# Attention stage: value matmuls of two k tiles issued together on even steps, denominator groups behind them, two reciprocals to a step

## What is computed

```python
att = jnp.einsum('bhgqd,bhkd->bhgqk', q, k) / scale
att = jax.nn.softmax(att, axis=-1)
y = jnp.einsum('bhgqk,bhkd->bhgqd', att, v)
```

## Time and profile before

| | |
|---|---|
| median of the runs | 3878.38 us |
| profiled execution, its own time | 3881.62 us |
| span in the trace | 3879.9 us |
| attention (first turn to last denominator group) | from 371 to 2257 us of the span |
| TensorE busy over the whole span | 3690.1 us (95%) |
| VectorE, ScalarE, GpSimd busy | 2415.0, 1732.0, 1627.1 us |

### The profile page before, as it was taken

How to read it: one execution, slowest core, us unless ns; L and a number is a source line. 1 busy time by engine, 2 the same in 40 slices (tenths; PEclk the granted TensorE clock), 3 DMA queues, 4 the chain that set the end, 5 groups by cost and what they waited for, 6 DMA issues and landing times. The chain is left out here.

```text
span 3879.9 us, 59156 instructions
## 1 busy us (share of the span) xinstructions
PE 3690.1 (95%) x19372; PEld 2401.0 (62%) x19372; DVE 2415.0 (62%) x4160; ACT 1732.0 (45%) x3071; POOL 1627.1 (42%) x549
## 2 busy tenths in 40 slices
PE   6998999999999999999999979799999999979889
PEld 4776444444444444444444358688888888868888
DVE  6433787777787777777777558544444444445554
ACT  3110466665666656666666633222222222125555
POOL 1111587787787777788788820000000000001110
PEclk8998899999999999999999999899999999999999
DMA  6654100101001010100100035711011111042121
GB/s 226 184 180 133 34 12 23 34 15 32 23 15 31 23 24 23 34 15 20 34 23 4 9 106 181 205 28 28 28 31 35 28 28 27 17 132 70 45 64 45
DMA packets 186866, 218.32 MB, mean 56 GB/s; under 512 B 29268, under 2 KB 148820, under 8 KB 182808
## 3 DMA queue, kind: packets, MB, share of 16 engines
q1 hardware_dynamic: 168488, 153.92, 14.3%
q0 software_dynamic: 15856, 59.52, 4.8%
q10 hardware_dynamic: 2304, 2.10, 0.2%
HBM read 152.70 MB, written 62.27 MB: 55 GB/s over the span
## 5 line engine op out<-in xcount | busy, mean ns | idle before, releaser
L689 DVE TENSOR_REDUCE att_chunk_max<-att_scores 128x1 f32<-128x512 f32 x2048 | 1284.7, 677 | 411.4 <-PE att_scores L760 404.2
L675 ACT ACTIVATE att_exp<-att_scores_T 128x512 f32<-128x512 f32 x2048 | 1122.3, 595 | 734.6 <-PE att_scores_T L774 716.3
L646 POOL TENSOR_TENSOR att_exp_pair<-att_exp 128x2048 f32<-128x2048 f32 x256 | 1169.5, 4579 | 440.7 <-ACT att_exp L675 440.7
L774 PE MATMUL att_scores_T<-att_q_stack,att_k_stack 98*128 98x512 f32 x2048 | 863.0, 424 | 13.1 <-ACT att_exp L675 9.6
L760 PE MATMUL att_scores<-att_k_stack,att_q_stack 96*128 96x512 f32 x2048 | 798.4, 436 | 40.2 <-DVE att_chunk_max L689 27.2
L774 PEld LDWEIGHTS att_scores_T<-att_q_stack,att_k_stack 98*128 98x128 f32 x2048 | 386.4, 189 | 497.8 <-ACT att_exp L675 290.4
L785 PE MATMUL att_y_acc<-att_exp,att_v_head 128*32 128x512 f32 x4096 | 547.9, 607 | 0.9 <-ACT att_exp L675 0.9
L760 PEld LDWEIGHTS att_scores<-att_k_stack,att_q_stack 96*128 96x128 f32 x2048 | 395.9, 193 | 245.2 <-DVE att_chunk_max L689 185.3
L1461 PE MATMUL down_acc<-dn_wd_hi,h_hi 128*128 128x256 f32 (+1 forms) x1408 | 369.8, 299 | 52.3 <-ACT h_hi L1382 37.1
L1140 POOL DMA_DIRECT2D inter_scratch<-gu_inter x84 | 45.2, 538 | 884.1 <-DVE gu_inter L1083 884.1
L1461 PE MATMUL down_acc<-dn_wd_lo,h_hi 128*128 128x256 f32 (+1 forms) x1408 | 355.2, 289 | 0.0
(11 more groups left out here) (185 smaller groups left out, 4749.1 us busy)
## 6 DMA issues: line engine op xcount, KB each, us to landing
att_q_stack<-q_scratch SPq DMA_DIRECT2D x96, 256.0 KB, 4.9
shared_raw<-in_wd_t SPq DMA_DIRECT2D x4, 2688.0 KB, 10.4
qkv_x_tile<-in_x SPq DMA_DIRECT2D x16, 512.0 KB, 4.8
q_scratch<-qkv_qk_out_hi POOLq DMA_DIRECT2D x32, 256.0 KB, 3.2
q_scratch<-qkv_qk_out_lo POOLq DMA_DIRECT2D x32, 256.0 KB, 4.2
qkv_wqkv_raw<-in_wmod POOLq DMA_DIRECT2D x8, 1024.0 KB, 7.6
qkv_wmod<-in_wmod POOLq DMA_DIRECT2D x8, 1024.0 KB, 8.2
y_scratch<-att_y_out SPq DMA_DIRECT2D x32, 256.0 KB, 2.4
```

Source lines behind the costliest of these rows:

```text
L646: nc.gpsimd.tensor_tensor(ps[PAIR_SLOT[j]][:], pr[2 * j % NP][:], pr[(2 * j + 1) % NP][:], ALU.add).then_inc(pair_done, 1)
L675: nc.scalar.activation(pr[k % NP][:, h * NB:(h + 1) * NB], stp[bank(GH * k + h)][:], ACT.Exp, scale=INV_SQRT_DH).then_inc(exp_done, 1)
L689: nc.vector.reduce_max(cmax[c % 2][:, q:q + 1], turn_buffer(u, q)[:], AX.X).then_inc(sm_done, 1)
L774: nc.tensor.matmul(stp[bank(i)][:], ks[c // QB % 2][0:SR + 2, k * P:(k + 1) * P], qs[c % 4][0:SR + 2, h, :], start=True, stop=True).then_i ...
```

## The change

Four edits in `stage_attention`:

- Value groups no longer run one to a step. On even steps k the groups of k-2 and k-1 are issued one behind the other, after the third transposed score and a turn. Odd steps have none. At step 0 they are the last two of the unit before.
- Denominator groups move from steps 13, 14, 15 and 0, 1, 2 to steps 10, 12, 14 and 0, 2, 4, each behind the two value groups.
- Reciprocals: two to a step on steps 5 to 8 (before: one to a step on steps 4 to 11). `y_out` follows in step 9 (before: 12).
- `copy_y` on ScalarE comes after the fourth exponential of step 0 (before: the second).

```diff
-    DEN_AHEAD = (13, 14, 15)
-    DEN_LATE = (0, 1, 2)
+    DEN_AHEAD = (10, 12, 14)
+    DEN_LATE = (0, 2, 4)
     RP = 8
-    RECIP_AT = 4
+    RECIP_AT = 5
+    RECIP_STEP = 2
...
-                        if k == 0 and h == 1 and not is_first(u):
+                        if k == 0 and h == GH - 1 and not is_first(u):
                             copy_y(u - 1, c - 1)
...
                         if i == 1 and not is_first(u):
-                            if RECIP_AT <= k < RECIP_AT + RP:
-                                recip(u - 1, k - RECIP_AT)
-                            if k == RECIP_AT + RP:
+                            if RECIP_AT <= k < RECIP_AT + RP // RECIP_STEP:
+                                for m in range(RECIP_STEP):
+                                    recip(u - 1, RECIP_STEP * (k - RECIP_AT) + m)
+                            if k == RECIP_AT + RP // RECIP_STEP:
                                 y_out(u - 1, c - 1)
...
                     ahead_turn()
                     scores_t(u, c, k, 1)
-                    if k > 0:
-                        by_v(u, c, g, k - 1)
-                    elif not is_first(u):
-                        by_v(u - 1, (c - 1) % BODY, g, KT - 1)
-                    if k in DEN_AHEAD:
-                        denominators(u, DEN_AHEAD.index(k))
-                    if k in DEN_LATE and not is_first(u):
-                        denominators(u - 1, len(DEN_AHEAD) + DEN_LATE.index(k))
+                    ahead_turn()
                     scores_t(u, c, k, 2)
                     ahead_turn()
+                    if k % 2 == 0:
+                        for b in (2, 1):
+                            if k > 0:
+                                by_v(u, c, g, k - b)
+                            elif not is_first(u):
+                                by_v(u - 1, (c - 1) % BODY, g, KT - b)
+                        if k in DEN_AHEAD:
+                            denominators(u, DEN_AHEAD.index(k))
+                        if k in DEN_LATE and not is_first(u):
+                            denominators(u - 1, len(DEN_AHEAD) + DEN_LATE.index(k))
+                    ahead_turn()
                     scores_t(u, c, k, 3)
-                    ahead_turn()
-                    ahead_turn()
...
-            by_v(NU - 1, (NU - 1) % BODY, HKV - 1, KT - 1)
+            for b in (2, 1):
+                by_v(NU - 1, (NU - 1) % BODY, HKV - 1, KT - b)
```

## The result

Five runs of the changed kernel have a median of 3897.70 us (3894.30 to 3901.74); five of the kernel before, 3878.52 us. The ratio is 1.0049, 95% interval 1.0034 to 1.0063: slower by half a per cent. The forecast was 3884 us, range 3845 to 3920. The profiled execution took 3894.3 us, 12.7 us more than that of before; it is the fastest of the five.

A forecast was written before the change was run, and what follows sets the result against it. Attention lasts as long as TensorE's queue, with VectorE timing one turn per step through three banks. A unit summed to 57.42 us, 0.27 longer; 29 units, first and last gave +5.9 on 3878.4: 3884 us, range 3845 to 3920.

The forecast's parts named there:

- ordinary pair of steps: Two steps with merged value groups: block 4.20 us behind the first turn plus 1.86, so 6.06 against 6.34 before.
- paired reciprocals, odd steps: VectorE, steps 5 and 7: two reciprocals behind turn 3 delay the block by 0.83 us each time, 1.66 a unit.
- `y_out`: VectorE, step 9: standing behind turn 3, it costs its slot of 0.61 us a unit; before, it was free.
- copy: ScalarE, step 0: the copy ahead of four exponentials makes transposed scores lag and the block 0.34 us later.
- step 14: At the maxima's transposition the block comes at 5.37 us, 1.17 later than 4.20; before, 1.15, so no difference.
- ScalarE's ring: Transposed scores between blocks: eight in some 3.6 us, near the 3.9 queued exponentials need; the last passes with 0.02 to spare.
- the merge pays in full: Rival: reciprocals, `y_out` and copy stay hidden, unit 54.81 us, kernel 3810, or 3848 with half hidden; chance 0.12 for both.
- Two groups still cost an exit each: Rival, TensorE: two value groups in a row each pay an exit, 0.14 us a pair more, kernel 3916; chance 0.07.
- The ring doesn't bind: Rival, three turn banks: turns stand further apart, blocks come at 3.95 us, unit 52.8, kernel 3752; chance 0.03.
- ScalarE's ring takes over: Rival, transposed scores' banks: exponentials 0.3 us later than walked move each block by 0.17, kernel 3923; chance 0.15.
- Unit 0: First unit, with neither reciprocals nor a copy: forecast 2.3 us shorter (-2.6 + 0.3).
- The last unit: Unit without turns, living on ScalarE's ring of banks: forecast 0.4 us longer.

The follow-up runs named there:

- e2: Changed kernel with reciprocals moved to steps 4, 6, 8 under the value blocks, `y_out` to step 10, last two denominator groups to steps 0, 2: 3832.3 us, ratio 0.9877.
- e1: Changed kernel with the ScalarE copy behind the third exponential of step 0 instead of the fourth: 3890.5 us, ratio 1.0028 to the kernel before.
- e3: Changed kernel with the transposed scores' bank repeat moved from the unit's last score to the first of step 7: 3883.3 us, ratio 1.0009 to the kernel before.
- e6: Changed kernel with each reduction over the first 256 of 512 columns and the exponent scaled to a sixteenth: 3786.9 us, ratio 0.9762 to the kernel before.
- e5: Kernel before with only two reciprocals to a step on steps 5 to 8 and `y_out` in step 9: 3882.3 us, ratio 1.0006.

## Why the prediction came out as it did

By its own steps, in us a unit:

| term | forecast | measured | from |
|---|---|---|---|
| ordinary pair of steps, eight times | 6.06 | 6.07 | e2, 1615.61 to 1621.68 |
| denominator groups | 6 x 0.86 | 6 x 0.86 | unchanged |
| paired reciprocals, odd steps | 2 x 0.83 | 2 x 0.80 | 1658.46 to 1665.33, less 6.07 |
| `y_out` | 0.61 | 0.60 | its pair 7.53, less 6.07 and 0.86 |
| copy | 0.34 | 0.34 | e1 |
| step 14 | 1.17 | 1.17 | steps 13 and 14 at 2.13 + 5.96, against 1.98 + 4.94 |
| end of the unit | 0 | 0.50 | e3 |
| unit | 57.42 | 57.92 | `y_out` starts |

The mechanism was right: the merge gave 6.34 - 6.07 = 0.27 a pair, not the 0.33 that TensorE's starts alone promise, and reciprocals, `y_out` and copy took it all back. e2 and e6 show that the chain of reductions is the cause, e5 that the old order did not charge for pairing.

One step of the walk failed: "ScalarE's ring". I looked for it in the middle of a unit, where three banks come round evenly, and took the pair of steps over the unit's end as an ordinary one with a denominator group. I had not followed `bank` to its exception. The sum had nothing for it; it cost 0.50 us in 29 to 31 units, some 15 us, and the miss was 14 us. It is not the rival that I gave 0.15: there, every pair was to be 0.17 longer, and the ordinary pairs are not.

The rivals: "the merge pays in full" came true only when the reciprocals were put elsewhere, at 3832 with those alone and 3809 with copy and repeat too, where I had priced it at 3810 (its unit of 54.85 was priced at 54.81). "Two groups still cost an exit each" fell by the 1.85 us of a block. "The ring doesn't bind" was approached only with shorter reductions (e6), and even so the unit was 54.62, not 52.8.

One sign was a bad one. I had written that the rival "ScalarE's ring takes over" holds if weight loads of transposed scores wait for exponentials in ordinary pairs. They do, 445 times in the changed kernel, in an ordinary pair for 0.19 us; but the same wait stood 317 times and 267.2 us in the kernel before, and the block of an ordinary pair still comes 4.21 behind its first turn (1683.95 - 1679.74 in the changed kernel), as the chain of reductions alone would have it. A load that waits need not hold up its matmul; the length of the pair decides.

Smaller sizes were off in the other direction, and in the total they hide part of the missed term.

- Unit 0, from its first transposed score to that of unit 1, went from 56.07 to 51.77: 4.3 us shorter, not 2.3. TensorE's granted clock was 0.50 (the 1.2 GHz level) when it began, with TensorE busy without a gap, and rose to 1.00 at 423.6 us before and at 420.8 after. In e3, which has the same unit 0 but for the bank, it rose at 423.8, and the unit took 52.94. So some 1.2 us of the 4.3 are the clock's. The other 3.1 hold one value group that no longer runs in unit 0.
- The last unit, to the end of the attention, went from 56.9 to 56.2, where I had added 0.4.
- Units 1 to 30, with the two places where the loop begins anew, took 21.4 us more, 1.7 less than 30 x 0.77.

That makes 21.4 - 4.3 - 0.7 = 16.4 us for the attention in the profiled executions (its end went from 2256.7 to 2273.2). The medians differ by 19.2 us, the profiled executions by 12.7. The stages behind the attention have the same code and were 4 us shorter in the profiled execution; with a spread of 7 us over five runs I leave that open.

## What to carry to other kernels

Merging bursts on the bound engine is priced by the walk from one burst to the next over each ring of buffers, not by the switches that it saves: the engines behind the rings must still fit their work between bursts, and whatever small work stands ahead of the item that the last slot waits for is paid in full, while the same work behind it, under the burst, is free. After such a merge look again at everything that was free before: e2 won 65 us by moving work of 2.3 us a unit a few places. And follow the buffer rotation over every exception and loop end, not only in its even part.

## What the runs showed of the hardware

- A group of four 32-column matmuls in plain fp32 (two passes) costs 0.86 us behind another such group, with other weights, and 1.00 alone; the entry and the first full-width matmul behind it cost 0.09 and 0.10 more. Two groups: 1.85.
- A reciprocal of 128x64 took a slot of 0.46 behind a reduction and 0.41 behind another reciprocal, against 0.60 for a queued reduction of 128x512; halving the reduction's columns brought its slot to 0.34 (e6). From these two an estimate of 0.08 us is left for no columns at all: a reduction's slot is nearly all in its columns. By the same line a reduction of 64 columns would take some 0.15 (an estimate), so the reciprocal is the dearer of the two for its size. Whether fewer and longer reciprocals would be cheaper, no run tells.
- The reduction right behind a reciprocal lasts 0.63 instead of 0.68, in all 240 cases of the kernel before and all 120 of the changed one, and the next queued one follows at 0.54 instead of 0.60. The prediction had this in its 0.83. What makes it shorter, no run tells.
